# Second cross attention: exponentials to SBUF, one instruction a plane, and the group evacuation before the high plane

## The reference

```
xn = _layernorm(x, ln_gamma, ln_beta)
q = (xn @ w_q).reshape(B, SQ, NUM_HEADS, DIM_HEAD)
k, v = jnp.split(context @ w_kv, 2, axis=-1)
scores = jnp.einsum('bqhd,bkhd->bhqk', q * SCALE, k)
attn = jax.nn.softmax(scores, axis=-1)
out = jnp.einsum('bhqk,bkhd->bqhd', attn, v).reshape(B, SQ, INNER)
out = (out @ w_out + b_out) * jnp.tanh(gate[0])
```

## Time and profile before

| | us |
|---|---|
| median of 3 runs | 2046.15 |
| lowest, highest | 2042.88, 2048.61 |
| the profiled execution | 2042.05 |
| its span, first to last instruction | 2040.3 |
| busy: TensorE | 1716.6 (84%) |
| busy: VectorE | 1540.6 (76%) |
| busy: ScalarE | 1186.4 (58%) |
| busy: GpSimd | 831.2 (41%) |

### The profile page before, as it was taken

One profiled execution on the slowest core, in us unless ns is written; L12 is line 12 of the kernel. 1 busy time (PEld: TensorE's weight loads), 2 busy tenths in 40 slices (PEclk: granted clock), 3 DMA queues, 4 the chain that ended last, 5 costly groups with the idle time before them and its releaser, 6 DMA issues. The chain is left out here.

```text
span 2040.3 us, 32726 instructions
## 1 busy us (share of the span) xinstructions
PE 1716.6 (84%) x9613; PEld 1220.6 (60%) x9613; DVE 1540.6 (76%) x2890; ACT 1186.4 (58%) x1868; POOL 831.2 (41%) x704
## 2 busy tenths in 40 slices
PE   4887887799954489999999999999999999985997
PEld 3554555788822356666666665665666666554886
DVE  4874765778857397888888788878888887865887
ACT  2432222777721277767777776777777777754453
POOL 4750111233333545354455536354544545321233
PEclk9987999799966599999999999999999999997998
DMA  5102774100000199999999999999999999981000
GB/s 195 68 0 79 291 301 185 42 1 0 1 0 0 55 209 204 211 196 207 193 203 188 210 192 206 204 197 204 193 207 190 206 192 209 187 170 70 2 8 10
DMA packets 722860, 290.13 MB, mean 142 GB/s; under 512 B 700892, under 2 KB 705020, under 8 KB 722044
## 3 DMA queue, kind: packets, MB, share of 16 engines
q1 hardware_dynamic: 722796, 289.36, 62.3%
HBM read 112.24 MB, written 0.92 MB: 55 GB/s over the span
## 5 line engine op out<-in xcount | busy, mean ns | idle before, releaser
L2179 DVE SCALAR_TENSOR_TENSOR xa_h<-xa_psum,xa_rinv,xa_h 128x500 f16<-128x500 f32 x672 | 452.6, 729 | 1.3 <-ACT xa_h L2278 1.3
L2278 ACT ACTIVATE xa_h<-xa_psum,xa_rinv 128x1000 f16<-128x1000 f32 x448 | 372.1, 882 | 126.1 <-DVE xa_rinv L2171 123.7
L2265 ACT ACTIVATE xa_psum<-xa_psum,xa_negmax 128x1500 f32<-128x1500 f32 x224 | 332.7, 1485 | 181.8 <-DVE xa_negmax L2164 181.2
L2160 DVE TENSOR_REDUCE xa_psum<-xa_psum 128x1 f32<-128x1000 f32 x224 | 270.5, 1208 | 180.7 <-PE xa_psum L2068 178.7
L2087 PE MATMUL xa_psum<-xa_prT,xa_n_hi 128*128 128x512 f16 (+1 forms) x768 | 273.6, 356 | 84.0 <-ACT xa_on L2245 72.2
L2066 PE MATMUL xa_psum<-xa_c_hi,xa_q_hi 128*128 128x500 f32 x672 | 285.0, 424 | 25.7 <-DVE xa_h L2179 9.7
L2088 PE MATMUL xa_psum<-xa_prT,xa_n_hi 128*128 128x512 f16 (+1 forms) x768 | 271.9, 354 | 0.0
L2089 PE MATMUL xa_psum<-xa_prT,xa_n_lo 128*128 128x512 f16 (+1 forms) x768 | 271.7, 354 | 0.0
L2067 PE MATMUL xa_psum<-xa_c_lo,xa_q_hi 128*128 128x500 f32 x672 | 261.6, 389 | 0.0
L2068 PE MATMUL xa_psum<-xa_c_hi,xa_q_lo 128*128 128x500 f32 x672 | 261.3, 389 | 0.0
L2087 PEld LDWEIGHTS xa_psum<-xa_prT,xa_n_hi 128*128 128x128 f16 x768 | 74.9, 98 | 196.9 <-issue 104.7
(11 more groups left out here) (299 smaller groups left out, 3439.4 us busy)
## 6 DMA issues: line engine op xcount, KB each, us to landing
ctxN<-in_ctxP SPq DMA_DIRECT2D x16, 1536.0 KB, 9.3
xa_ctxP<-in_ctxP SPq DMA_DIRECT2D x32, 768.0 KB, 4.8
ctxT<-in_ctxT SPq DMA_DIRECT2D x16, 1500.0 KB, 6.3
xa_ctxT<-in_ctxT SPq DMA_DIRECT2D x32, 750.0 KB, 5.0
xa_prT<-xa_h SPq DMA_TRANSPOSE x224, 5.7
up<-in_F_up SPq DMA_DIRECT2D x1, 2048.0 KB, 9.2
down<-in_F_down SPq DMA_DIRECT2D x1, 2048.0 KB, 13.3
gate<-in_F_gate SPq DMA_DIRECT2D x1, 1024.0 KB, 4.8
```

The source lines that it names most:

```text
L2160: nc.vector.tensor_reduce(psum[:, bank + 1, W:W + 1], psum[:, bank:bank + 2, 0:W], AX.XY, ALU.max)\
L2179: nc.vector.scalar_tensor_tensor(h[:, H_SLOT[s], 1, a:z], psum[:, bank + j, 0:W], rinv[:, s % 2, :], h[:, H_SLOT[s], 0, a:z], ALU.mult, AL ...
L2265: nc.scalar.activation(psum[:, bank:bank + 3, 0:W], psum[:, bank:bank + 3, 0:W], ACT.Exp, bias=negmax[:, s % 2, :], accum_out=rs[:, s % 2, ...
L2278: nc.scalar.activation(h[:, H_SLOT[s], 0, a * W:z * W].rearrange("p (a c) -> p a c", c=W), psum[:, bank + a:bank + z, 0:W], ACT.Identity, ...
```

## The change

A new tensor `p`, [128, 2, 1500] in fp32, lies in SBUF with one slot for even and one for odd units. `exponentials` writes there instead of over the scores, and first waits until the low part of unit s - 2 has read its slot. `high_part` and `low_part` become one instruction each over 1500 columns, both read `p`, and `h1_ready` and `h2_ready` count units instead of pieces. `scores` waits once, for `exp_ready` of unit s - 2. `evacuate` moves behind `exponentials` of the step in which its group's values end, ahead of `keep_q` and `high_part`. The scratch space for GpSimd's DMAs shrinks, which makes room for `p`.

```diff
--- before.py
+++ after.py
@@ -1852,6 +1852,7 @@
         ctxT, ctxP = sb("ctxT", [128, C]), sb("ctxP", [128, CP])
         c_hi, c_lo = sb("c_hi", [128, 2, C], fp32r), sb("c_lo", [128, 2, C], fp32r)
         n_hi, n_lo = sb("n_hi", [128, 2, CP], fp16), sb("n_lo", [128, 2, CP], fp16)
+        p = sb("p", [128, 2, C])
         h = sb("h", [128, 4, 2, CP], fp16)
         prT = sb("prT", [128, 2 * GA + UPS - GA, 2 * KT, 128], fp16)
         negmax, rs, rinv = sb("negmax", [128, 2, 1]), sb("rs", [128, 2, 1]), sb("rinv", [128, 2, 1])
@@ -1930,7 +1931,7 @@
 
             def transpose(i, s):
 
-                sp.wait_ge(h2_ready, this(i, 3 * s + 3, 3 * NU))
+                sp.wait_ge(h2_ready, this(i, s + 1, NU))
                 sp.sem_inc(issuing, 1)
                 b, u = s // UPS, s % UPS
 
@@ -2059,9 +2060,9 @@
                     pe.wait_ge(c_lo_ready, this(i, b + 1, 2))
                 qh = q_hi[:, b, p0:p0 + UQ, :].rearrange("p a b -> p (a b)")
                 ql = q_lo[:, b, p0:p0 + UQ, :].rearrange("p a b -> p (a b)")
+
+                pe.wait_ge(exp_ready, this(i, s - 1, NU))
                 for j, (a, z) in enumerate(PIECES):
-
-                    pe.wait_ge(h2_ready, this(i, 3 * (s - 2) + j + 1, 3 * NU))
                     out = psum[:, bank + j, 0:W]
                     nc.tensor.matmul(out, qh, c_hi[:, b, a:z], start=True, stop=False)
                     nc.tensor.matmul(out, qh, c_lo[:, b, a:z], start=False, stop=False)
@@ -2150,7 +2151,7 @@
         @block.vector
         def _(dve):
             open_sems(dve, NU, two_ready, max_ready, total_ready, rinv_ready)
-            open_sems(dve, 3 * NU, h2_ready)
+            open_sems(dve, NU, h2_ready)
             t.open_vector(dve)
 
             def maximum(i, s):
@@ -2171,13 +2172,10 @@
                 nc.vector.reciprocal(rinv[:, s % 2, :], total[:, s % 2, :]).then_inc(rinv_ready, 1)
 
             def low_part(i, s):
-                bank = 3 * (s % 2)
                 dve.wait_ge(rinv_ready, this(i, s + 1, NU))
-                for j, (a, z) in enumerate(PIECES):
-                    if j != 1:
-                        dve.wait_ge(h1_ready, this(i, 2 * s + (1 if j == 0 else 2), 2 * NU))
-                    nc.vector.scalar_tensor_tensor(h[:, H_SLOT[s], 1, a:z], psum[:, bank + j, 0:W], rinv[:, s % 2, :],
-                                                   h[:, H_SLOT[s], 0, a:z], ALU.mult, ALU.subtract).then_inc(h2_ready, 1)
+                dve.wait_ge(h1_ready, this(i, s + 1, NU))
+                nc.vector.scalar_tensor_tensor(h[:, H_SLOT[s], 1, 0:C], p[:, s % 2, :], rinv[:, s % 2, :],
+                                               h[:, H_SLOT[s], 0, 0:C], ALU.mult, ALU.subtract).then_inc(h2_ready, 1)
 
             def residual(i):
 
@@ -2229,7 +2227,7 @@
         def _(act):
             open_sems(act, NB, q_kept)
             open_sems(act, NU, exp_ready)
-            open_sems(act, 2 * NU, h1_ready)
+            open_sems(act, NU, h1_ready)
             open_sems(act, NG, on_kept)
             t.open_scalar(act)
             act.wait_ge(on_zeroed, 1)
@@ -2262,11 +2260,12 @@
             def exponentials(i, s):
                 bank = 3 * (s % 2)
                 act.wait_ge(max_ready, this(i, s + 1, NU))
-                nc.scalar.activation(psum[:, bank:bank + 3, 0:W], psum[:, bank:bank + 3, 0:W], ACT.Exp,
+
+                act.wait_ge(h2_ready, this(i, s - 1, NU))
+                nc.scalar.activation(p[:, s % 2, :].rearrange("p (a c) -> p a c", c=W), psum[:, bank:bank + 3, 0:W], ACT.Exp,
                                      bias=negmax[:, s % 2, :], accum_out=rs[:, s % 2, :]).then_inc(exp_ready, 1)
 
             def high_part(i, s, first):
-                bank = 3 * (s % 2)
 
                 earlier = [x for x in range(s) if H_SLOT[x] == H_SLOT[s]]
                 if earlier:
@@ -2274,18 +2273,16 @@
                 elif not first:
                     act.wait_ge(transposed[max(x for x in range(NU) if H_SLOT[x] == H_SLOT[s])], i * 16)
                 act.wait_ge(rinv_ready, this(i, s + 1, NU))
-                for a, z in ((0, 2), (2, 3)):
-                    nc.scalar.activation(h[:, H_SLOT[s], 0, a * W:z * W].rearrange("p (a c) -> p a c", c=W),
-                                         psum[:, bank + a:bank + z, 0:W], ACT.Identity, scale=rinv[:, s % 2, :])\
-                        .then_inc(h1_ready, 1)
+                nc.scalar.activation(h[:, H_SLOT[s], 0, 0:C], p[:, s % 2, :], ACT.Identity, scale=rinv[:, s % 2, :])\
+                    .then_inc(h1_ready, 1)
 
             def step(i, s, first=False, end=False):
-                at = evacuation_at(*unit(i, s - 1))
-                if at and (s > UPS or not first):
-                    evacuate(*at)
                 if s == STORE and not first:
                     t.scalar_store(act, i - 1, 0, psum[:, 7, 128:256])
                 exponentials(i, s)
+                at = evacuation_at(i, s)
+                if at and (s > UPS or not first):
+                    evacuate(*at)
                 if s in PROJECT and not end:
                     keep_q(i + 1, PROJECT[s])
                 high_part(i, s, first)
@@ -2295,8 +2292,8 @@
                     keep_q(0, c)
 
             def epilogue():
-                for s in range(-1, UPS):
-                    at = evacuation_at(*unit(PAIRS, s))
+                for s in range(UPS):
+                    at = evacuation_at(PAIRS, s)
                     if at:
                         evacuate(*at)
                 t.scalar_store(act, PAIRS - 1, 0, psum[:, 7, 128:256])
@@ -2490,7 +2487,7 @@
     from concourse.bass_utils import run_bass_kernel_spmd
 
     arrays = {"in_" + name: a for name, a in layouts({n: np.asarray(v) for n, v in inputs.items()}).items()}
-    nc = bacc.Bacc("TRN2", target_bir_lowering=False, num_devices=1)
+    nc = bacc.Bacc("TRN2", target_bir_lowering=False, num_devices=1, dynamic_dma_scratch_size=2048)
     dram = {}
     for name, a in arrays.items():
         ap = nc.dram_tensor(name, list(a.shape), fp32, kind="ExternalInput").ap()
```

## The result

The kernel after took 2112.62 us (median of four runs, 2109.68 to 2118.77), the kernel before beside it 2047.38 (2042.88 to 2049.09). The ratio is 1.0326, with a 95% interval from 1.0297 to 1.0355. The predicted 2105 was 7.6 us short and the range held the time. The profiled execution took 2109.68, its span 2107.9; predicted were 2101 for it.

What follows compares the result with a forecast made beforehand. No engine was full; VectorE's chain with port waits would set the pace: 57.1 + 14.2 + 2.8 = 74.1 us a pair against 70.56. Together +59 on 2042.05 gives 2101, and the median 4.1 above gives 2105; range 2035 to 2165.

Steps and rivals of the forecast that it cites:

- VectorE's own chain: Second cross attention, light step: VectorE's work without waiting falls from 4.15 to 3.99 us, 57.1 us a pair.
- The port: Low parts with two SBUF inputs wait for GpSimd instructions reading SBUF: 14.2 us a pair, all on VectorE's chain.
- Rival B: GpSimd's scaling lets VectorE through, so some 4.3 us a pair go: pair 69.8 us, kernel 2036; chance 0.05.
- four terms: Low parts' waits in GpSimd's bursts: 0.6 and 2.4 us (queries, context), 1.7 and 2.1 (values); 6.8, twice 13.6 a pair.
- the 1.2 and 0.6 us: Port cost a pair: 1.2 added for bursts beginning within a gap, 0.6 hidden by the chain's slack at 8 hits.
- Rival A: The port doesn't matter for low parts: pair at 65.2 us, kernel 1963; chance 0.10.
- Rival D: DMA engines at 97%: transposes set the pace and the gains vanish without any port, kernel 2046; chance 0.02.
- C: Half of the 8 hits meet a long GpSimd instruction just begun, some 5 us a pair more: 2180; chance 0.04.
- Evacuation: Moved into ScalarE's gap, it frees bank 6 about when TensorE finishes the next scores: 5.2 us a pair of waiting go.
- this tie: Values after an evacuation cannot run ahead, so heavy steps go at TensorE's pace: VectorE keeps 2.8 us a pair of waiting.
- Waits for scores: VectorE's waits for TensorE's scores fall from 10.2 us a pair to about 3, with 2.8 in the sum.
- GpSimd, held, is idle half its time: nothing: GpSimd, held 1.8 us a hit by low parts, has idle time enough, so its delay costs nothing.

Runs made afterwards that it cites:

- e3: Kernel before with evacuation moved and one instruction a plane, but exponentials kept in PSUM, so the low part has one SBUF input: 2144.53 us.
- e1: Kernel after, low part replaced by a maximum over p with one SBUF input, low plane left zero: 1961.12 us.
- e6: Kernel after, GpSimd's split instructions replaced by zero fills that only write SBUF: 1954.42 us.
- e4: Kernel after with the group evacuation back at the start of the next step: 2161.67 us.
- e2: Kernel before with only the group evacuation moved behind the exponentials, which stay in PSUM: 1983.13 us.
- e5: Kernel after with each of GpSimd's seven kinds of split instructions cut into four: 2059.29 us.

## Why the prediction was right, and where its steps were off

**Lengths.** The low part was put at 1.80 us (1.74 to 2.02): 1.770, and the same from PSUM (e3). Exponentials 1.52: 1.513. High plane 1.49: 1.539, not on the chain. VectorE's own chain, 3.99 a light step: 3.98 in e1 and e6. That it is the same with a low part of 1.71 us and of 1.77 fits the prediction, in which the exponentials and not the low part decide when the total can start.

**The port.** Predicted 14.2 us a pair, measured 14.2 in the fourteen middle pairs. Here are three meetings in the kernel after, for the first two VectorE's rows and then GpSimd's beside them, and for the third its low part and the scaling (start, length):

```profile
1293.43 3.25 DVE L2177 SCALAR_TENSOR_TENSOR xa_h<-xa_p,xa_rinv,xa_h 128x1500 f16<-128x1500 f32 x1
...
1298.89 4.12 DVE L2177 SCALAR_TENSOR_TENSOR xa_h<-xa_p,xa_rinv,xa_h 128x1500 f16<-128x1500 f32 x1
...
1293.00 2.09 POOL L1989 TENSOR_TENSOR xa_q_lo<-xa_q_full,xa_q_hi 128x896 fp32r<-128x896 f32 x1
1295.04 2.93 POOL L1998 CAST xa_c_hi<-xa_ctxT 128x1500 fp32r<-128x1500 f32 x1
1298.05 3.40 POOL L2000 TENSOR_TENSOR xa_c_lo<-xa_ctxT,xa_c_hi 128x1500 fp32r<-128x1500 f32 x1
...
1230.05 2.59 DVE L2177 SCALAR_TENSOR_TENSOR xa_h<-xa_p,xa_rinv,xa_h 128x1500 f16<-128x1500 f32 x1
...
1227.61 4.35 POOL L2007 TENSOR_SCALAR xa_ctxP<-xa_ctxP,xa_n_scale 128x1536 f32<-128x1536 f32 x1 [1.27 <-DMA xa_ctxP<-in_ctxP]
```

The first low part ends at 1296.68; less its 1.77 it began to work at 1294.91, 0.18 before the recorded end of GpSimd's subtraction. The cast that GpSimd had next took 2.93 us instead of 1.44: it was held while the low part worked, until 1296.7. The second low part began to work at 1301.24, 0.21 before the end at 1301.45. Both end about 1.6 us after the GpSimd instruction that they waited for (1.59 and 1.56), as the prediction had said of the long ones. The wait is the rest of the instruction that runs: 1.48 and 2.35 us here. This holds for all 93 low parts that waited for a subtraction; with unrounded times they began to work 0.19 to 0.20 us before its recorded end.

The scaling is different, and the prediction did not have this. The third low part began to work at 1230.87, and the scaling ended at 1231.96: 1.09 us later. In all 31 meetings with a scaling it is 1.07 to 1.08 us with unrounded times, and the low part ends 0.7 after the scaling and not 1.6. So the last microsecond of this GpSimd instruction does not hold VectorE. In e4, fourteen low parts even began in that stretch and took 1.77 us. Why, no run shows.

**Rival B** (the scaling lets VectorE through) is refuted, but for that last microsecond. Of the 224 low parts 124 were held. By the GpSimd instruction for which they waited, 32 were held by the values' subtraction (2.17 us on average), 31 by the context's (2.34), 30 by the queries' (1.38), and 31 by the scaling (1.14). The prediction had 2.1, 2.4, 0.6 and 1.7. Two of its four terms are right; the queries' is less than half of what was measured and the scaling's half as much again, and these misses, with the 1.2 and 0.6 us that it added and took off, cancel. That the port came out to the tenth is luck; its four meetings of 1.1 to 2.3 us, twice a pair, are not. **Rival A** (the port doesn't matter) is what e1 and e6 make of the kernel by taking the port away: 1961 and 1954 where I had 1963, with a pair of 64.4 to 64.6 where I had 65.2. **Rival D** (transfers set the pace at 97%) fell there as well: the view's DMA share of 0.97 was no ceiling, it went to 1.06 and the pair to 64.43. **C** (fresh long instructions at half of the hits, +5 us a pair) did not happen: 14.2 in all.

**Evacuation: the step that failed.** The prediction put TensorE's 5.2 us at bank 6 at nothing after the move. That is so in e2, where the pair fell by 4.25 us. In the kernel after two waits a pair stayed, 4.5 us, close to the 5 that the prediction had named as a sign of being wrong. When the bank comes free was right: 2.24 us after the start of the exponentials (1240.99 to 1243.23 at the longer wait), predicted 2.35. Where TensorE is then was wrong. The prediction had it just done with the next scores, but it had done them at 1239.12, 4.1 us before. The evacuation now stands behind the exponentials, those behind the maximum, and that behind the low part in VectorE's queue, and the low part ahead of this one was held: it took 3.95 us. I had this tie in the sum only with its 2.8 us, and not what happens to it in a step that the port stretches. Since VectorE sets the pace, TensorE, busy 67.08 of 75.11 us, must stand somewhere for 8 us a pair, and as such a standing costs nothing. What this one cost is the clock.

**Waits for scores.** Predicted 2.8 us a pair left, measured 4.5 in this pair and 4.1 on average. What was missing is the clock. TensorE in the kernel after, around the longer of the two waits, then three stretches before, at and behind it in the columns of the earlier trace rows:

```profile
1243.23 0.50 PE L2088 MATMUL xa_psum<-xa_prT,xa_n_hi 128*128 128x384 f16 x1 [4.10 <-ACT xa_on L2243]
...
1247.05 1.77 PE L2052 MATMUL xa_psum<-x_feat,key_query 128*128 x8
...
1250.70 0.34 PE L2088 MATMUL xa_psum<-xa_prT,xa_n_hi 128*128 128x384 f16 x1
...
1252.66 1.04 PE L2052 MATMUL xa_psum<-x_feat,key_query 128*128 x8
...
1234.90:1241.70 6.80, 4.23 (x23) 2.98 (x21) 6.64 (x6) 3.85 (x4) 2.26 (x1) 1.00 0.74 141
1241.70:1248.50 6.80, 5.27 (x19) 3.43 (x20) 5.09 (x8) 5.09 (x8) 0.00 (x0) 0.50 1.10 240
1248.50:1255.30 6.80, 6.80 (x40) 5.29 (x39) 4.07 (x6) 5.28 (x8) 0.00 (x0) 1.00 0.85 170
```

TensorE did nothing for over 4 us, then worked for 5.3 us at 1.2 GHz (0.50) and was back at 2.4 GHz (1.00) from 1248.5 on. The values' 12 products took 1247.05 - 1243.23 = 3.8 us at the lower level and 1252.66 - 1250.70 = 2.0 at the full one; the quarter of a projection 1.77 and 1.04. Together that is some 2.5 us. So the scores of the next step came late, and VectorE stood in the middle of a pair in which it is the bound:

```profile
1250.21 1.21 DVE L2161 TENSOR_REDUCE xa_psum<-xa_psum 128x1 f32<-128x1000 f32 x1 [2.77 <-PE xa_psum L2069]
```

The other pairs show that these 2.77 us are the clock's. The time that TensorE works at the lower level after this standing differs from pair to pair, from 2.96 us in the fourth to 5.66 in the fifth, and VectorE's wait goes with it, from 1.65 to 2.94. Over the fourteen pairs a straight line through them has a slope of 0.50 us of wait for each us of work at half clock, and 0.13 us of wait are left where there is none. The average wait is 2.37, so 2.2 us a pair are the clock's, and this is port time at second hand: stretched low part, late evacuation, idle TensorE, halved clock, late scores. The other two waits of the pair, 0.85 us each, are the tie in the heavy steps, predicted at 0.9.

**"GpSimd, held, is idle half its time: nothing"** was right for this kernel, with GpSimd busy for 41 of 75 us; at 56 (e5) the sum at the end of its queue set the pace of the last steps.

**The sum.** In each of the fourteen middle pairs the length less held time and waits for scores is 57.0 to 57.4 us; the prediction's chain was 57.1. So the average pair is 57.1 + 14.2 + 4.1 = 75.4 where the prediction had 57.1 + 14.2 + 2.8 = 74.1, and its whole miss there is the waits for scores: 2.2 us from the clock, less about 1 of the predicted waits that did not come. Fourteen times this is +18 us. The first pair was put at +9 and is +4.2: held time is as elsewhere (15.3), but the pair has no residual and its steps take 3.85 us without held time (53.9 in place of 57.1), and 2.4 us of its held time fall behind its end. The last with what follows was put at about +0.5 and is -3.1; its held time is 4.5 us, where the prediction left 11. So 8 to 9 us come back, and the rest is under 1 us. The predicted +59 and the measured +67.6 are as near as they are partly by luck: the misses of the first and last pair ran against that of the others.

**What stays open.** Which meeting falls where in a pair (steps of 4.2 to 7.1 us in the pair above, most of them repeating from pair to pair) was not worked out. In the pairs with the shorter wait the held time is up to 1.4 us longer, so that the pair is not shorter; what a kernel without the fall of the clock would take was not run. The gain of 22 to 29 us from merging and earlier banks is a difference of kernels with the port out of play; in the kernel as it is, it can't be seen by itself.

## What to carry to other kernels

Before a tensor moves from PSUM to SBUF, count the SBUF inputs of every VectorE instruction that reads it. If one gets its second, its price here was the rest of the SBUF-reading GpSimd instruction that runs at its start (for the scaling the rest less 0.9 us), on VectorE's chain, so look how long GpSimd's instructions are against VectorE's gaps. Cutting the few long ones gives most of it back (here held low parts went from 219 us to 48, and with all cut to 29), but look first at what stands behind them in GpSimd's queue. And a change of two parts needs both built alone: here one line's place was worth 3%, and the rest of the edit hid it.
